# A fused two-layer block on one core: the first cross-attention cut into tiles of 32 channels by 4 batches

## What is computed

```python
x = x + tanh(g_xattn[0]) * L0_xattn(ctx, ctx, layernorm(x), ssm_kernel, D, head_dim=8)
x = x + tanh(g_ffn[0])   * L0_ffn(layernorm(x))        # int8 weights and rows, one scale for all rows
x = x + tanh(g_xattn[1]) * L1_xattn(layernorm(x), ctx) # softmax attention, a batch at a time
x = x + tanh(g_ffn[1])   * L1_ffn(layernorm(x))        # ternary weights

# L0_xattn(k, v, q, ...): 32 heads of 8 channels, every batch
kv  = einsum('bhil,bhjl->bijhl', k, v)                 # products of channel pairs
y   = causal_convolution(kv, ssm_kernel[h]) + kv * D[h]
out = einsum('bijhl,bhil->bjhl', y, q)

# L0_ffn: quant_per_tensor(x) divides by ONE maximum over all of x
# _ternary_quant(w): needs the mean of |w| over the whole matrix first
```

## Time and profile before

| | us |
|---|---|
| device time, median of 3 runs | 643.41 (643.09 to 644.05) |
| span of the profiled execution | 641.4 |
| PE busy | 611.9 |
| DVE busy | 544.2 |
| ACT busy | 483.0 |
| POOL busy | 346.5 |

### The profile page before, as it was taken

One profiled execution on the slowest core, in us unless ns is written; L12 is line 12 of the kernel. 1 busy time (PEld: TensorE's weight loads), 2 busy tenths in 40 slices (PEclk: granted clock), 3 DMA queues, 4 the chain that ended last, 5 costly groups with the idle time before them and its releaser, 6 DMA issues.

```text
span 641.4 us, 9520 instructions
## 1 busy us (share of the span) xinstructions
PE 611.9 (95%) x2863; PEld 362.3 (56%) x2894; DVE 544.2 (85%) x1065; ACT 483.0 (75%) x725; POOL 346.5 (54%) x430
## 2 busy tenths in 40 slices
PE   5899999999999999989999999999888999999997
PEld 5677777777776445544445556555433444444443
DVE  2697888889999788986779988889898999999964
ACT  4469785766655898998672576776679999999984
POOL 2579888888874255210001111114488988898861
PEclk9999999999999999999999999999999999999999
DMA  8959896899999355128538920000115665666651
GB/s 301 377 195 305 297 317 225 266 333 341 333 296 314 135 196 197 66 61 306 219 79 177 229 91 16 16 17 1 55 44 151 189 185 174 171 180 166 181 161 51
DMA packets 127862, 118.92 MB, mean 185 GB/s; under 512 B 83456, under 2 KB 90384, under 8 KB 126672
## 3 DMA queue, kind: packets, MB, share of 16 engines
q1 hardware_dynamic: 120384, 104.23, 52.8%
q10 hardware_dynamic: 7440, 14.24, 6.5%
HBM read 68.04 MB, written 30.49 MB: 154 GB/s over the span
## 4 chain that ended last, share of the span: by engine, by line
PE 65%; DVE 13%; ACT 11%; issue 6%; DMA 2%; POOL 1%; SPq 0%; ACTq 0%; DVEq 0%; POOLq 0%
PE ps L1189 22%; PE ps L1484 14%; PE ps L1500 8%; PE ps L1309 5%; ACT turn L975 4%; PE ps L1411 3%; PE ps L1441 3%; DMA arena<-in_x 2%; ACT arena L920 2%; PE ps L1459 2%; PE ps L1415 2%; PE ps L1198 2%; PE ps L1391 1%; PE ps L1401 1%; DVE turn L1878 1%
## 5 line engine op out<-in xcount | busy, mean ns | idle before, releaser
L1189 PE MATMUL ps<-arena 128*128 128x288 f32 x640 | 160.6, 407 | 2.0 <-DVE inv_s L1671 0.8
L1189 PEld LDWEIGHTS ps<-arena 128*128 128x128 f32 x640 | 119.4, 190 | 34.1 <-issue 1.0
L1484 PE MATMUL ps<-arena 128*128 128x512 bf16 x510 | 113.4, 379 | 4.1 <-DVE arena L2073 4.0
L1484 PEld LDWEIGHTS ps<-arena 128*128 128x128 bf16 x512 | 49.6, 98 | 65.9 <-issue 4.1
L687 POOL TENSOR_TENSOR arena<-arena 128x512 f32<-128x512 f32 x64 | 80.3, 1275 | 8.9 <-DVE arena L2073 8.0
L585 POOL TENSOR_TENSOR arena<-arena 128x1024 f32<-128x1024 f32 x32 | 60.6, 1893 | 16.7 <-issue 11.5
L1500 PE MATMUL ps<-arena 128*128 128x512 bf16 x241 | 57.1, 379 | 1.9 <-ACT arena L1089 0.7
L1309 PE MATMUL ps<-arena 128*128 128x512 bf16 (+1 forms) x248 | 56.2, 379 | 0.9 <-ACT arena L920 0.4
L1353 PE MATMUL ps<-arena 128*128 128x512 bf16 x250 | 55.3, 379 | 0.7 <-DVE arena L1822 0.4
L592 POOL TENSOR_TENSOR turn<-turn 128x512 f32<-128x512 f32 x31 | 40.5, 1305 | 23.5 <-DVE turn L1648 23.5
L2073 DVE SCALAR_TENSOR_TENSOR arena<-ps,up_scale,arena 128x512 f32<-128x512 f32 x64 | 46.7, 745 | 5.8 <-ACT arena L1065 5.0
(11 more groups left out here) (233 smaller groups left out, 1296.1 us busy)
## 6 DMA issues: line engine op xcount, KB each, us to landing
arena<-in_L_ffn_w SPq DMA_DIRECT2D x48, 512.0 KB, 6.3
arena<-kpad_d ACTq DMA_DIRECT2D x16, 512.0 KB, 7.1
hq_d<-arena SPq DMA_DIRECT2D x14, 512.0 KB, 2.7
tern_d<-late SPq DMA_DIRECT2D x24, 256.0 KB, 5.6
arena<-in_ctx SPq DMA_DIRECT2D x4, 1024.0 KB, 12.1
arena<-in_x SPq DMA_DIRECT2D x4, 1024.0 KB, 14.8
arena<-in_L_ffn_w ACTq DMA_DIRECT2D x8, 512.0 KB, 6.0
arena<-in_ctx SPq DMA_DIRECT2D x2, 2048.0 KB, 10.4
```

Source lines behind the costliest of these rows:

```text
L1189: last = pe.matmul(ps[:, 4 * s + lo, 0:NB * PAIRS], toep[:, u, (LB - 1 - lo + li) * P:(LB - lo + li) * P], kv[:, s, li, :], start=(li == 0 ...
L1484: last = pe.matmul(ps[:, bank, :], xq4T[:, s, 4 * j + k, :], w[:, k, c * L:(c + 1) * L], start=(k == 0), stop=(k == LB - 1))
```

## The change

Tiles of `x_res`, `ctx` and `qT` in the first cross-attention (and up to the feed-forward stage) become 32 channels x 4 batches. Two such tiles hold 4 heads of all 8 batches. Tile pair g serves heads 4g to 4g+3.

- Loads: each pair of tiles is four DMAs of 32 partitions x 2 rows x 2 KB (128 KB each); 4 of them are issued by ACT, the rest by SP, which after 8 of them waits until the padded kernel is stored (`k_stored`). The last eight tiles of `x` come in eight DMAs of 256 KB.
- Start: 13 ctx tiles and 2 q tiles are transposed ahead of or between head 0's matmuls and behind them, before head 1. Head 1's matmuls follow ctx tile 12, the tile of the last of those loads. DVE makes the first pairs.
- Heads 1 to 17 each transpose one further tile; heads 18 to 31 (`FIRST_TURN` = 18) each turn one tile back, DVE adds it and takes statistics one head later. Two tiles (14, 15) are left behind head 31. The copies of `x_res` into PSUM are gone.
- Statistics of `x` are taken one tile a head, in heads 0 to 9, the first of these waiting for all remaining tiles of `x`.
- The mean of each of the three weight matrices is taken by itself, in heads 11, 17 and 25 (`MEAN_AT`); before, it was one wait between heads 15 and 16. Two of the four int16 to bf16 widenings of the first layer's weights go from DVE to ACT (heads 23 and 27), one more from DVE to POOL.
- Both 2 MB loads of `ctx_early` are issued as soon as the last `repeat_c` is done and the stream's last item was used. `theta` is made entirely ahead of the maximum: three batches before the last two tiles are turned back, five after.
- A group of the feed-forward stage is now every second tile, so the additions run over tiles 8, 10, 12, 14, then 9, 11, 13, 15, then 0, 2, 4, 6, then 1, 3, 5, 7. `attn_stats` and `attn_x` move accordingly. The 4 stores of 1 MB of `x1_d` become 16 of 256 KB, from 32 partitions each.

```diff
-        order1 = [t for half in range(TB) for t in range(half, NT, TB)]
+        order1 = [2 * (G * (n % 2) + n // 2 % G) + n // NB for n in range(NT)]
-        FIRST_TURN = 20
+        opening = [("c", n) for n in range(6)] + [("q", 0), ("q", 1)] + [("c", n) for n in range(6, 13)]
+        late = [None] + [("q", n) for n in range(2, 6)] + [("c", n) for n in range(13, NT)] + [("q", n) for n in range(6, NT)]
+        FIRST_TURN = len(late)
+        SUM_AT, MEAN_AT = (9, 15, 23), (11, 17, 25)
```

SP, its loads at the start and behind the heads:

```diff
-            load_ctx(0)
-            load_ctx(1)
-            load_x(0)
-            load_x(1)
-            load_ctx(2)
-            load_x(2)
-            load_x(3)
-            load_ctx(3)
+            load_x(0, x_in[0])
+            load_ctx(sp, 1, c_in[1])
+            sp.wait_ge(S["k_stored"], 16)
+            load_ctx(sp, 2, c_in[2])
+            load_ctx(sp, 3, c_in[2])
+            load_x(1, x_in[1])
+            load_x(2, x_in[1])
...
+            load_ctx(sp, 4, c_in[3])
+            load_ctx(sp, 5, c_in[3])
+            load_ctx(sp, 6, c_in[4])
+            load_ctx(sp, 7, c_in[4])
+            load_x(3, x_in[2])
+            load_x_late(x_in[2])
...
             sp.wait_ge(S["cd_ready"], HEADS)
-            sp.dma_start(ctx_early[0], ctx_rows[:, 0:NT // 2, :]).then_inc(c_in[1], 16)
-            sp.wait_ge(S["prod_done"], HEADS + 2)
-            sp.dma_start(ctx_early[1], ctx_rows[:, NT // 2:NT, :]).then_inc(c_in[2], 16)
+            sp.dma_start(ctx_early[0], ctx_rows[:, 0:NT // 2, :]).then_inc(c_in[0], 16)
+            sp.dma_start(ctx_early[1], ctx_rows[:, NT // 2:NT, :]).then_inc(c_in[1], 16)
+            for m in range(2, WC // 2):
+                w1_turned(m)
```

More of the change, by code:

```diff
@@ new lines, in _ @@
+            copied("q", 0)
+            copied("q", 1)
+            repeat_q(0, 0)
+            repeat_c(2, 0)
+            for m in range(8, len(opening)):
+                open_copy(m)
+            act.wait_ge(S["th_tr"], 1)
+            act.activation(b1[:, :], ps[:, open_bank(len(opening)), 2 * P:2 * P + FT], ACT.Copy)
+            act.activation(th_w.rearrange("p d k -> p (d k)"), ps[:, open_bank(len(opening)), 0:2 * P], ACT.Copy).then_inc(S["th_made"], 1)
+            x_normal(2)
+            x_normal(3)
@@ new lines, in open_tiles, with warm_up @@
+            def open_tiles(part):
+                for m in part:
+                    src = tile_in(*opening[m])
+                    if m >= 6:
+                        opened(pe, m - 4)
+                    for l in range(LB):
+                        last = pe.transpose(ps[:, open_bank(m), l * P:(l + 1) * P], src[:, l * P:(l + 1) * P], identf[:, :])
+                    last.then_inc(S["open_tr"], 1)
+            def warm_up(times):
+                for n in range(times):
+                    pe.transpose(ps[:, 7, n % 4 * P:(n % 4 + 1) * P], identf[:, :], identf[:, :])
@@ L1185, in head @@
+            warm_up(16)
+            open_tiles(range(2))
+            warm_up(12)
+            open_tiles(range(2, 4))
+            def head(h, turned):
+                s, u = h % 2, h % 4
+                if h - 2 in MEAN_AT:
+                    pe.wait_ge(S["binv_ready"], MEAN_AT.index(h - 2) + 1)
                 pe.wait_ge(S["kv_ready"], h + 3)
@@ L1191, in head @@
                                          kv[:, s, li, :], start=(li == 0), stop=(li == lo))
[L1192 to L1196 removed]
+                    if h == 0 and lo == 2:
+                        open_tiles(range(4, 8))
+                if h in MEAN_AT:
+                    w = MEAN_AT.index(h)
+                    pe.wait_ge(S["bsum_ready"], w + 1)
+                    pe.matmul(ps[:, 4 * s, 416 + w:417 + w], mean_w[:, :], scol[:, w:w + 1], start=True, stop=True)
@@ new lines, in _ @@
+                head(h, turned)
+                if h == 0:
+                    open_tiles(range(8, len(opening)))
+                    pe.wait_ge(x_in[NG - 1], 32)
+                    at = open_bank(len(opening))
+                    opened(pe, len(opening) - 4)
+                    for d in range(2):
+                        pe.transpose(ps[:, at, d * P:(d + 1) * P], th_raw[:, d, :], identf[:, :])
+                    pe.transpose(ps[:, at, 2 * P:2 * P + FT], b1n, identf[0:FT, 0:FT]).then_inc(S["th_tr"], 1)
@@ L1282, in theta @@
                 last.then_inc(S["th_tr"], 1)
-            for b in range(G + 1):
+            for b in range(3):
+                theta(b)
+            pe.wait_ge(S["o_done"], 2 + HEADS)
+            pe.wait_ge(S["prod_done"], 2 + HEADS)
+            pe.wait_ge(S["x1_dve"], TAIL)
+            for n in range(TAIL, NT):
+                for l in range(LB):
+                    last = pe.transpose(ps[:, 4 + n - TAIL, l * P:(l + 1) * P], back_rows(n, l), identf[:, :])
+                last.then_inc(S["back_tr"], 1)
+            for b in range(3, NB):
                 theta(b)
@@ L1313, in _ @@
             rows_T(0)
-            theta(G + 2)
-            theta(G + 3)
-            pe.wait_ge(S["w1_ready"], 4)
-            for f in range(G):
-                pe.wait_ge(S["th_made"], G + f + 2)
-                mm1(0, (f,))
+            pe.wait_ge(S["w1_ready"], 2)
+            pe.wait_ge(S["th_made"], NB + 1)
+            mm1(0, range(G))
             rows_T(1)
```

724 lines of the change are left out of this document (338 added, 386 removed).

## The result

The changed kernel takes 668.84 us (668.33 to 669.24, 4 runs) against 643.38 (643.09 to 644.05, 4 runs) before: a ratio of 1.0392, 95% interval 1.0377 to 1.0407, so 25.5 us slower. The forecast of 645.5 and its range up to 653 were wrong. The profiled execution has a span of 666.8.

A forecast was written before the change was run, and what follows sets the result against it. PE, busy 95% of the span, was taken as the bound, so savings count in its work or waits. Terms -1.9 + 3.5 - 1.1 + 1.6 = +2.1 gave a span of 643.5, 645.5 as median; range 639.5 to 653.

The forecast's parts named there:

- The start, -1.9 us: Up to head 1: loads at 409 GB/s, head 1 at 27.0 instead of 28.86, so 1.9 us saved.
- loads into 32 partitions are slow: Rival for the loads at the start: each DMA covers a quarter of the partitions and moves slower; 655 us, chance 0.20.
- the wait for the stored kernel: Start: SP waits for the padded kernel's store, taken as 2.6 us, so SP goes on at 6.1 (bounds 5.7 and 9.5).
- SP's pitch of 0.48 us: Start: SP needs 0.48 us to issue each DMA, whatever its size; 34 DMAs take 16.3 us.
- each microsecond beyond about 33 costs one: Start: DVE's tile 6 statistics wait for all of x; landing beyond about 33 us costs one for one.
- Heads, +3.5: Heads 1 to 31 on PE: seven more tiles transposed within heads, 167.1 us against 163.6, so 3.5 us slower.
- E to the first layer, -1.1: From E (PE's end of head 31) to the resumed `mm1`: 3.4 us saved, 2.3 lost again to theta waiting for ctx.
- three theta ahead of the last transposes: Behind head 31: three theta products (5.25 us) wait for ctx at E + 2.9 and end at E + 8.2.
- DVE's way to the maximum: From DVE's last head to the maximum: 17.0 us instead of 18.46, maximum at E + 21.0 without the theta wait.
- Behind the maximum, part of the same -1.1: Maximum to resumed `mm1`: theta gone from PE, `mm1` at +4.7 instead of +7.1, the resumed one at E + 30.2.
- Seam, +1.6: Seam to the second attention: DVE waits 0.8 for ACT's copy and 0.8 for POOL's scale, 1.6 us slower.
- Rest, 0: First feed-forward stage, attention loop and last stage keep their instructions and durations: no change.

The follow-up runs named there:

- e3: Changed kernel with each load of 32 partitions laid over 128 partitions, same size and number (other channels in the tiles, so only its time counts): 660.35 us.
- e1: Kernel before, each 1 MB load of ctx and x cut by partitions into four DMAs of 32 partitions x 4 rows: 651.64 us, ratio 1.0134.
- e2: Kernel before, each 1 MB load of ctx and x cut by rows into four DMAs of 128 partitions x 1 row: 643.25 us, ratio 1.0001.
- e6: Changed kernel with each ctx tile loaded by one DMA of 128 partitions, 32 channels outermost in the source; x loads unchanged: 664.40 us.
- e14: e12 with statistics of the fourteen tiles turned back within heads taken over 64 of 512 positions: 651.44 us.
- e12: e6 plus DVE's statistics of tiles 6 to 9 in heads 2 and 3, e11's tail, and POOL's second-group scales made before the same head's products: 653.86 us.
- e7: Changed kernel with the last two tiles turned back before all theta; ACT copies one theta ahead of the last normalisations, seven behind: 661.59 us.
- e11: e7 with 38 dummy transposes of the identity in PE's idle time behind head 31: 659.19 us.
- e8: Kernel before, with statistics and normalisations of batches 0 and 1 at the seam moved to the changed kernel's places: 645.20 us, ratio 1.0031.
- e4: Changed kernel with each tile loaded by one DMA of 128 partitions, 4 batches outermost in the source: 720.22 us.
- e9: e6 with x loads for partitions 64 to 127 issued by ACT, those for 0 to 63 by SP: 667.28 us.

## Why the prediction was wrong, step by step

- **The start, -1.9 us: wrong, the largest error.** The failed step is "at the 409 GB/s of the stream ... they land at about 31.5", and with it head 1 at 27.0, whose last ctx tile I had landed at 24.6. No load of 32 partitions was in the trace of before, and I carried over the rate of loads over 128. They move at 215 to 237 GB/s in the fence above; all x came at 46.6, and the shape alone is 9.9 us (e3). The rival "loads into 32 partitions are slow" had the mechanism, and even the place (head 3 at 51.5, measured 51.73), and the rule of the Trainium skill quoted there ("SBUF — State Buffer", "Door 1: The DMA port swizzle") held for 32 partitions: 221 against 379 GB/s in e1 and e2. I gave it 0.20 because DMAs to different quarters might overlap. Within one queue they do not (233 GB/s in e6 with x alone); this reason against the rule had no row behind it. Even this rival's upper end, 659, was 10 us short, for the reasons in the next points. The start had a second, smaller fault: with the fast shape it still gives +1.9 up to head 3 and not -2.4 (e3), since I took the wait for the stored kernel too short and the transposes at full clock.
- **SP's pitch of 0.48 us: right** (0.47). The wait for the stored kernel held SP for 4.2 us, its store taking 4.9 for my 2.6; behind such loads it was no longer what set the end; with fast ones it would have been part of it (e3).
- **"each microsecond beyond about 33 costs one": right.** By it, x at 46.6 puts head 3 at 51.2; it came at 51.73. Within that, the gate cost 1.4 us ahead of head 3, on top of head 1's own delay; what I had not seen is that ctx tile 12, by the same slow loads, would hold head 1 back by itself.
- **Heads, +3.5: sign and mechanism right, size short by 1.1** (+5.1 for +4.0 from head 3 on). Heads 18 to 31 took 5.56 and not 5.41: DVE's statistic and add (e14), and POOL's late scales (e12). Heads with a forward tile took 5.29 as forecast.
- **E to the first layer, -1.1: wrong.** I had the right object, three theta ahead of the last transposes, and the wrong sizes. ctx landed at E + 5.5, not E + 2.9, and that is the issue (205.03 in SP's timeline, E - 4.3 for my E - 7.2: the stream's last item was used at 204.6, ACT having waited 4.45 us for POOL's scales), not the load, 9.7 us for my 10.1. Then three theta took 7.64 for 5.25, behind 5.5 us of idle PE and at a lowered clock. The transposes were at E + 13.0 and not E + 8.2, the maximum at E + 27.1 where I had 23.3 with the same wait. The prediction took every duration from rows at full clock. e7 and e11 give 7.2 and 2.4 us back. DVE's way to the maximum was right: without the wait it came at E + 21.1 in e7. (I wrote E + 21.0; the terms as listed sum to 17.3 and not 17.0, which makes it 21.3.)
- **Behind the maximum, part of the same -1.1: wrong by 2.9.** From the maximum to the resumed `mm1` I had 9.2 us, since theta (three batches stood there before, six matmuls in the order rows, not four) was gone from PE; it took 12.15, longer than the 11.2 before. PE now idles between the steps, and its records ran slower: the 16 transposes took 1.86 us where they took 1.05 before, and the first `mm1` 5.54 where it was 3.40. The granted clock was 0.50 from 237 to 242.3 and 0.61 from there to 247.8; before, it was 1.00 from 210 to 230. e7 and e11 leave this gap as it is; filling it, or leaving theta there, was not tried.
- **Seam, +1.6: right** (+1.8 here, +2.0 by itself in e8), by the two waits named.
- **Rest, 0: +1.2 measured**, behind `gx_copy`; in the last stage PE idles 3.5 us ahead of its L1521, 1.6 of it for a DMA, where the same matmul had 1.9 before. Why these DMAs come later was not tried.

## What to carry to other kernels

Cut a load by rows, not by partitions: here DMAs into 32 neighbouring partitions each ran at little more than half the rate, although the next one went to the next quarter. When a layout needs several source blocks in one tile, put the long dimension outermost in the source (32 channels here, not 4 batches) and let the partitions interleave. Where a trace has no row for a shape of transfer, a guess that its effect overlaps is worth less than a rule that says it doesn't. And price what stands behind a new wait of PE at a lowered clock as well, and look for filler or real work to put into it. Work that seems to be in the way between two short steps of PE (theta behind the maximum) may be what keeps its clock up.

## What the runs showed of the hardware that was not expected

- A DMA of 128 partitions whose source has 4 batches outermost uses 4 of 16 engines: 102 GB/s, share 0.26 (e4). The same tile with 32 channels outermost: 351 GB/s, with some loads of x among them (e6).
- 32-partition loads that rotate over the four quarters within one queue move 215 to 237 GB/s with the DMA engines busy throughout (the changed kernel), 221 in e1 against 379 by rows in e2; 311 to 339 when two queues held them (e9, perhaps not a pure stretch).
- In the stretch from 215 to 225, behind 6.3 us of idle PE, the granted clock was 0.81 (e7); with 4.3 us of dummy transposes in the gap it was 1.00 (e11), and the kernel 2.4 us faster in the median.
